# A graph layer's edge sums: 32-column strips placed by one matmul, and eight dense blocks instead of five

## The reference

```
x: (6250, 256); src, dst: 200000 edges, dst sorted; edge_weight
dst = int(6250 * u**2), u uniform; src uniform
xn = layernorm(x)
gnn:  xn @ W_self + segment_sum((xn @ W_neighbor)[src] * edge_weight, dst) + bias
mix:  linear attention: q, k, v = xn @ w_qkv (8 heads of 64), k and v normalised per head,
      out = q @ (k.T @ v) / N @ w_out + b_out
x = x + gnn + mix
x = x + ffn(layernorm(x))        # 8 experts, top 2, hidden 1024
```

## Time and profile before

| | |
|---|---|
| median of 3 runs | 2875.6 us (2859.43 to 2879.97) |
| span of the profiled execution | 2417.9 us |
| PE, PEld busy | 2142.0 us (89%), 1814.8 us (75%) |
| DVE, ACT, POOL busy | 1326.0 us (55%), 788.0 us (33%), 1489.1 us (62%) |
| DMA | 273.02 MB, mean 113 GB/s |

### The profile page before, as it was taken

One profiled execution on the slowest core, in us unless ns is written; L12 is line 12 of the kernel. 1 busy time (PEld: TensorE's weight loads), 2 busy tenths in 40 slices (PEclk: granted clock), 3 DMA queues, 4 the chain that ended last, 5 costly groups with the idle time before them and its releaser, 6 DMA issues. The chain is left out here.

```text
span 2417.9 us, 50110 instructions
## 1 busy us (share of the span) xinstructions
PE 2142.0 (89%) x11532; PEld 1814.8 (75%) x11533; DVE 1326.0 (55%) x3807; ACT 788.0 (33%) x2485; POOL 1489.1 (62%) x1637
## 2 busy tenths in 40 slices
PE   6699977887789989988988896958999999999998
PEld 5477766666677666766766685947999999999998
DVE  7788867465584776676577454683222222222222
ACT  4355524122341432332243000333333333333332
POOL 2377777777777777777777775013545545545544
PEclk9799999999999999999999998579999999999999
DMA  8533334643346335534634664761222222222222
GB/s 284 166 105 106 107 108 120 180 126 105 108 125 198 110 110 173 149 110 133 189 109 125 191 206 121 250 243 25 37 37 35 37 37 35 37 37 35 37 37 33
DMA packets 160182, 273.02 MB, mean 113 GB/s; under 512 B 29900, under 2 KB 115660, under 8 KB 159788
## 3 DMA queue, kind: packets, MB, share of 16 engines
q0 software_dynamic: 78480, 195.05, 30.8%
q1 hardware_dynamic: 81632, 77.16, 9.9%
HBM read 232.65 MB, written 39.45 MB: 113 GB/s over the span
## 5 line engine op out<-in xcount | busy, mean ns | idle before, releaser
L847 POOL DMA_INDIRECT big<-support_d,big x1088 | 1060.7, 975 | 323.7 <-issue 292.8
L1244 PE MATMUL psBB<-big 128*128 128x256 f32 x2176 | 556.8, 413 | 140.0 <-DMA big<-support_d,big 111.7
L1244 PEld LDWEIGHTS psBB<-big 128*128 128x128 f32 x2176 | 444.1, 207 | 251.5 <-issue 181.5
L1747 POOL DMA_INDIRECT out<-accs,sidx x104 | 233.8, 2248 | 294.1 <-DVE accs L1821 246.3
L1077 DVE TENSOR_SCALAR R_<-big 128x196 f32<-128x196 f32 x761 | 271.9, 393 | 107.1 <-PE psD L1275 84.5
L1046 DVE TENSOR_SCALAR big<-big 128x128 f32<-128x128 f32 x1088 | 296.0, 365 | 0.0
L1853 PE MATMUL psBB<-accs 128*128 128x128 f32 x1664 | 195.4, 276 | 0.0
L1853 PE MATMUL psC<-accs 128*128 128x128 f32 x1664 | 194.3, 275 | 0.0
L1853 PEld LDWEIGHTS psBB<-accs 128*128 128x128 f32 x1664 | 191.1, 193 | 0.0
L1853 PEld LDWEIGHTS psC<-accs 128*128 128x128 f32 x1664 | 190.0, 192 | 0.1
L1863 PE MATMUL psD<-big,accs 128*128 x832 | 188.2, 379 | 0.0
(11 more groups left out here) (324 smaller groups left out, 2861.6 us busy)
## 6 DMA issues: line engine op xcount, KB each, us to landing
big<-support_d SPq DMA_DIRECT2D x140, 128.0 KB
big<-support_d,big POOLq DMA_INDIRECT x1088
big<-w POOLq DMA_DIRECT2D x16, 1024.0 KB, 11.7
sup_s_<-support_d SPq DMA_DIRECT2D x105, 128.0 KB
big<-xnT_d SPq DMA_DIRECT2D x98, 128.0 KB
out<-accs SPq DMA_DIRECT2D x7, 896.0 KB, 4.2
xnT_d<-R_ SPq DMA_DIRECT2D x36, 128.0 KB, 1.9
accs<-x POOLq DMA_DIRECT2D x5, 896.0 KB, 10.6
```

What stands on the lines that cost most here:

```text
L847: nc.gpsimd.indirect_dma_start(out=G[:, s, t, :], out_offset=None, in_=support_d, in_offset=bass.IndirectOffsetOnAxis(ap=idxs[:, s * GT + ...
L1244: last = nc.tensor.matmul(psBB[:, bank, 0:D], S[:, s % SETS * GT + t, :], G[:, s, t, :], start=(t == 0), stop=(t == GT - 1))
L1747: nc.gpsimd.indirect_dma_start(out=out, out_offset=bass.IndirectOffsetOnAxis(ap=sidx[:, b.s:b.s + 1], axis=0), in_=y[:, b.s, :], in_offset ...
```

## The change

**Strips.** A group's eight columns of edges are four strips of two. Each strip spans fewer than 32 nodes, so its one-hot is 128x32 against the strip's own base node, and its product goes to 32 of the 128 output lanes. ScalarE copies the 128 x 256 result to SBUF (`take_group`), and one product with a 0/1 matrix (`spread`) puts the lanes in their places (`finish`), into the other bank. VectorE makes all eight one-hots in one comparison and one multiplication of 128x256. GpSimd now waits for `strips_done`, and the zero matmuls go. A group with a strip of 32 nodes or more, or 128 and more in all, is left out (its bases are moved by `ASIDE`) and summed column by column in a loop at the end, which runs once on padding if there is none.

**Tables.** The first stage finds lowest and highest node per strip and not per group (16 transposes instead of 4, 22 small products instead of 5, about 25 more operations on at most 98 x 8 elements); four passes over all 1568 columns that put the lanes apart go. The tables of windows have 256 entries instead of 160.

**Order.** 8 dense blocks instead of 5, with 6 rounds in block 0 and 3 in each other (one group in each turn, four at the end), 6 key/value tiles in each block and 7 in the last; then 1 round beside the mixing and the rest alone. ScalarE copies the group of a turn before it goes on with the columns of that turn's later windows.

```diff
-HEAVY = 5
+HEAVY = 8
-HALVES = ((0, 8, (2, 2)),)
-STAGES = ((0, 1, ((0, 8, (4,)),), 2, 6), (1, 2, ((0, 4, (4,)), (4, 8, (2, 2))), 2, 4), (2, HEAVY - 1, HALVES, 2, 3),
-          (HEAVY - 1, HEAVY, HALVES, 1, 3))
-ROUNDS_MIX = 2
+NARROW = 32
+STRIPS = P // NARROW
+SPLIT = GT // STRIPS
+KV_BLOCK = 6
+QUARTERS = ((0, 4, (1, 1, 1, 1), (1, 0, 1, 1)), (4, 8, (1, 1, 1, 1), (0, 1, 0, 1)))
+STAGES = ((0, 1, ((0, 6, (2, 2), (0, 1)), (6, 8, (4,), (1,))), 1, 6), (1, 2, QUARTERS, 1, 4), (2, HEAVY - 1, QUARTERS, 1, 3), (HEAVY - 1, HEAVY, QUARTERS, 2, 3))
+ROUNDS_MIX = 1
...
                         wait_apart(pool,
                                    (idx_ready, i * 2 + s // 2 + 1),
-                                   (group_used, i * RING + s + 1))
+                                   (strips_done, i * RING + s + 1))
...
+                def take_group(s, n):
+                    wait_apart(act,
+                               (strips_done, n + RING),
+                               (node_done, n))
+                    nc.scalar.activation(strips[:, s % SETS, :], strip_sums, ACT.Copy).then_inc(strips_taken, 1)
...
+                    if kt is not None:
+                        square(kt)
+                    for q in range(PER_TURN):
+                        if brings(sums, q):
+                            take_group(*groups.pop(0))
+                        if q == 1 and kt is not None:
+                            root(kt)
+                        while ahead <= min(q + 2, len(quads)) and (ahead - 1 <= q or not brings(sums, ahead - 1)):
+                            select_source(ahead % PER_TURN, u, *quads[ahead - 1])
+                            ahead += 1
+                        if q % 2:
+                            evict(b, q // 2, b * TURNS + j, j)
...
-                        for t in range(GT):
-                            c = s * GT + t
-                            nc.vector.tensor_scalar(S[:, s % SETS * GT + t, :], index[:, 0:P],
-                                                    cols[:, 0, c:c + 1], cols[:, 1, c:c + 1],
-                                                    ALU.is_equal, ALU.mult).then_inc(s_ready[t], 1)
+                def select_node(s, g, n, block, lane):
...
+                    dve.wait_ge(strips_done, n + RING - SETS)
+                    nc.vector.tensor_tensor(mine, iota[:, 0:NARROW].unsqueeze(1).to_broadcast(shape),
+                                            dst_wts[:, 0, bass.ds(c, GT)].unsqueeze(2).to_broadcast(shape),
+                                            ALU.is_equal).then_inc(found, 1)
+                    dve.wait_ge(node_done, n)
+                    nc.vector.tensor_scalar(spread[:, x, :], turning[:, bass.ds(within(dve.snap(turned), 1, P), P)], place[:, bass.ds(g + s, 1)], None,
+                                            ALU.is_equal).then_inc(spread_ready, 1)
+                    dve.wait_ge(found, n)
+                    nc.vector.tensor_tensor(mine, mine, dst_wts[:, 1, bass.ds(c, GT)].unsqueeze(2).to_broadcast(shape),
+                                            ALU.mult).then_inc(s_ready, 1)
...
+                def sum_group(s, full, n):
+                    pe.wait_ge(gathered[s], full)
+                    pe.wait_ge(strips_taken, pe.snap(n + SETS - 1))
+                    pe.wait_ge(s_ready, pe.snap(n))
+                    for i in range(SPLIT):
+                        for q in range(STRIPS):
+                            t = q * SPLIT + i
+                            last = nc.tensor.matmul(strip_sums[q * NARROW:(q + 1) * NARROW, :], S[:, s % SETS * GT + t, :],
+                                                    G[:, s, t, :], start=(i == 0), stop=(i == SPLIT - 1))
+                    last.then_inc(strips_done, 1)
+
+                def finish(s, full, n):
+                    pe.wait_ge(strips_taken, pe.snap(n + SETS))
+                    pe.wait_ge(spread_ready, pe.snap(n))
+                    pe.wait_ge(ps_free, pe.snap(n + 1))
+                    nc.tensor.matmul(node_sums, spread[:, s % SETS, :], strips[:, s % SETS, :],
+                                     start=True, stop=True).then_inc(node_done, 1)
```

More of the change, by code:

```diff
@@ L639, in _ @@
+                step(nc.vector.tensor_reduce(rall[:, 1:2], wide, AX.X, ALU.add))
+                step(nc.vector.tensor_scalar(mtab[0:1, GROUPS + 1:], rall[:, 1:2], 1.0, None, ALU.max))
                 norms(25, 28)
@@ L929, in _ @@
+                rounds = within(act.snap(act.snap(ROUNDS - r0) & MASK), LIGHT_LEAST, ROUNDS)
+                with act.Fori(ROUNDS_HEAVY, rounds) as r:
+                    for group in groups_from(r):
+                        take_group(*group)
             @block.vector
@@ L1236, in sum_group @@
-                def sum_group(s, full, first, end):
-                    with pe.Fori(first, end) as n:
-                        own = pe.snap(n + 1)
-                        pe.wait_ge(ps_free, own)
-                        bank = within(odd(n), 0, 1)
-                        pe.wait_ge(gathered[s], full)
-                        for t in range(GT):
-                            pe.wait_ge(s_ready[t], own)
-                            last = nc.tensor.matmul(psBB[:, bank, 0:D], S[:, s % SETS * GT + t, :],
-                                                    G[:, s, t, :], start=(t == 0), stop=(t == GT - 1))
-                        last.then_inc(pair_used, 1)
@@ L1248, in free_group @@
[L1248 to L1254 removed]
+                    return [(s, full, r * RING + s + 1) for s in range(RING)]
```

563 lines of the change are left out of this document (352 added, 211 removed).

## The result

The changed kernel is slower: 3016.9 us (median of 4 runs, 3016.4 to 3024.0) beside 2872.9 us for the kernel before, ratio 1.0525, interval 1.0487 to 1.0563. The forecast was 2800 us.

The account below looks back on a forecast made before the run. GpSimd's indirect gathers (1.286 us each) were taken to bound the graph stage. Graph stage -84 us, tail +6 and first stage +2 gave -76, so 2875.6 us became about 2800, range 2715 to 2900.

Parts of the forecast that it names:

- 457.7 more: Whole run: median 2875.6 us less profiled span 2417.9 us, taken to lie around the span and stay unchanged.
- -76 us: Whole kernel: graph stage -84 us, behind the last gather +6, first stage +2; span from 2417.9 to 2342 us.
- Gathers removed: Graph stage on GpSimd: 960 gathers instead of 1088 at 1.286 us, -164.6 us if GpSimd kept its pace.
- Strips: TensorE, per group of 1024 edges: eight strip products partly overlapping in 1.95 us, 2.7 us with waits, copy and placement.
- The turn: Later dense blocks: 12.9 us with a key/value tile, 8.05 without, 11.1 on average, 11.3 taken; a block 133 us.
- Who sets the pace: Later dense blocks: turns of 11.3 us where gathers want 10.3; GpSimd waits for strip products some 10 us a block.
- gathers keep their pace: Rival, graph stage: the forecast's chains are too long and GpSimd stays the bound, 2725 us; chance 0.13.
- The other stretches: Graph stage: block 0 268 us, block 1 150, six blocks 798, light groups 99; 1315 us against 1399.2.
- Before and behind: First stage +2 us, bounds -5 and +8; behind the last gather +6 us for copy, placement and the wide-group loop.
- Serial strips: Rival, TensorE: each strip product uses the array alone, 3.46 us a group, 156 us in all, 2956 us; chance 0.2.
- All four at once: Rival, TensorE: strip sums take the 0.87 us bound, a block 129 to 130 us, 2765 us; chance 0.12.
- Lock-step over ScalarE: Rival: TensorE waits 1 to 1.5 us more per turn for columns behind ScalarE's copy, 2865 to 2895 us; chance 0.1.

Follow-up runs that it names:

- even series: Kernels run after each other on one chip, where the unedited kernel before takes 2417 to 2424 us; the profile behind the prediction is like one.
- held: Kind of series in which the unedited kernel before takes 2810 to 2880 us and register and branch instructions of several engines are slow.
- half gathers: Kernel before with every other gather left out from the second round on: 2243.0 us beside 2421.7, and 2288.4 us beside 2822.5 in the slower kind of series.

## Why the prediction was wrong, point by point

**The step that failed** is the last of the sum: "457.7 more, which lies around the span and isn't changed". One profiled execution stood 16% under the median of the runs, and its stage of gathers was taken for that of the runs. The section on the time and profile before says the same of the runs' times, and both are wrong: in every run since, a span is its run's time less 1 to 3 us. The gap of a sixth was itself the hint that the profile was of another kind of execution. The rest of the sum, -76 us, was right in its sign where it can be tested: in an even series the change gave -45.4 us (2373.8 - 2419.2). The forecast was therefore of another execution than the one measured, and none of the rivals had in it that all engines could be held up. A block then costs what it costs with its streams held: 59 to 79 us on top in a later block of the changed kernel, 50 to 61 in one of before.

Why before loses less per block can be read off the half gathers: its other engines need 175 us for a block and its gathers 203 to 205, so up to 30 us of delay are hidden in every block; in the changed kernel they need 124 and the gathers 3 x 32 x 1.286 = 123.5, and nothing is. 55 + 30 = 85 against 77: the delay itself is about the same per block. This is argued from these lengths, not tested by itself.

**Gathers removed: right.** 960 of them, 1.286 us each as before. Even, the stage from first to last gather went from 1398.2 to 1339.2, -59.0 where -84 was forecast.

TensorE's waits for their data went from 111.7 to 65.1 us, none of it in blocks 1 to 7.

**Strips: wrong in size, on the good side.** 1.95 us was assumed. TensorE of the changed kernel, even, a turn with a key/value tile in order of time:

```profile
842.76 1.07 PE L1431 MATMUL psBB<-big 128*32 128x256 f32 x16
843.96 0.17 PE L1444 MATMUL psD<-zeros 128*128 128x1 bf16 x1
844.31 1.26 PE L1461 MATMUL psD<-R_,big 128*128 128x196 f32 x6 [0.18 <-issue]
845.40 0.60 PE L1439 MATMUL psBB<-big 128*128 128x256 f32 x2
...
847.61 1.26 PE L1461 MATMUL psE<-R_,big 128*128 128x196 f32 x6 [0.40 <-ACT big L1005]
849.18 1.26 PE L1461 MATMUL psE<-R_,big 128*128 128x196 f32 x6 [0.32 <-ACT big L1005]
...
854.81 1.07 PE L1431 MATMUL psBB<-big 128*32 128x256 f32 x16
```

Sixteen records in 1.07 us where the earlier trace rows has 3.63: all four strips run at once, the bound of 0.87 and a little. The Trainium skill (TensorEngine Tiling (Array Packing), Tiling Modes) has this, and the trace agrees; of the drain at each change of mode that the page also names, the trace shows at most the 0.13 us between the strips' end and the next product.

**The turn: 12.0 us with a tile (842.76 to 854.81) where 12.9 was forecast.** The waits for ScalarE's columns are there (0.40 and 0.32) and small. ScalarE's copy was right (0.38), VectorE's broadcasts too (0.42 and 0.43 against 0.44). A later block came to 124.2 instead of 133.

**Who sets the pace.** The forecast had GpSimd wait some 10 us a block for strip products. In the last five blocks it waits 3.0, 2.3, 0.3, 1.2 and 2.0 us, and four of them are as long as their gathers (123.5 us): there the rival "gathers keep their pace" was right. With half of the gathers such a block takes the same 124 us, so the other engines' chain happens to be equally long, and the forecast's 133 us for it was too long. GpSimd's waits for the strips, 111.3 us in the whole stage, lie elsewhere: 26.8 in block 0, 5.1 in block 1, 32.3 in block 2 (which has 39 turns of three columns and took 152.9 us) and 38.2 behind the last block.

**The other stretches, even.** Block 0 took 290.0 us, 22 more than forecast; its window tables were priced right (two operations of 4.4 us). Block 1 147.5 (150), the six others 781.5 (798), the rest 121.1 (99): there GpSimd is not "at pace" but waits for TensorE, which sums a group only between two lots of 25 mixing tiles:

```profile
ACT big L989 <- PE psBB L1431: 118.9, 11, 28.1
DVE accs L1166 <- PE psBB L1439: 45.6, 9, 9.4
POOL big L938 <- PE psBB L1431: 38.2, 4, 18.6
```

That is the table of waits from 1322 to 1443 us; one wait of GpSimd is 18.6 us long. Blocks 0 and the rest give back +44, the six blocks and block 1 take 19.

**Before and behind.** The first stage was put at +2 us with a bound of +8: the first gather starts at 102.9 instead of 94.5, +8.4. Behind the last gather, from its start to the last add, 9.8 us instead of 13.0; from there to the first expert output 168.6 instead of 161.7, the +6 forecast for the loop over wide groups. Sum: -59.0 + 8.4 - 3.2 + 6.9 = -46.9 us, against -76.

**Rivals.** Serial strips: no. All four at once: yes as a mechanism; it was to give 2765. Gathers keep their pace: in the later blocks, not over the stage. Lock-step over ScalarE: about 10 us a block, held, and only at a block's end; its reading of the earlier trace rows has a slip, since the fifth block's clock of 0.94 stood beside TensorE busy for 88% of the time and not 85%. A reader of the result alone might take it for one of the two that forecast 2865 or more (serial strips, lock-step); it was neither.

**What stays open.** What in a gather holds up the other engines' register instructions, and why only in some series. It shows only where gathers and dense blocks run together: at the end of the stage gathers go out beside the mixing with next to no slow instruction, and the experts' stage has as many instructions, 36 GB/s of transfers and none at all. Many transfers by themselves aren't enough: right behind the last gather, held, 197 GB/s are moved without a slow instruction. Whether the gather's instruction or its rows matter wasn't seen, since the run that would have told came even. Nor is it known whether these instructions run slowly or arrive late; the two runs on the length of loop bodies test only that length. A page of the Trainium skill (NOTIFIC — the notification-queue block, Overflow: three behaviours, one of which stalls the engine) says that the block which writes an engine's notification records can hold the engine up when its own pipeline backs up; that would fit a cause common to several engines, but GpSimd, whose records go there too, has next to no slow instruction, and no run here tests it.

No version beats both kernels in both kinds of series: six and eight blocks are 2% ahead of before even, and in a held series the strips with five blocks are the best that was measured (0.7%). Six blocks weren't seen held.

## What to carry to other kernels

Before anything is priced from a profile, its span has to match the runs that will be the measure; where it is a sixth shorter, find the missing time first. A plan that trades a slower-looking engine's work for more instructions on all the others is only worth its price where those instructions cost what the profile says, and slack behind the bound is worth something when they don't. And when an engine's pace seems to set a block, take half of its work away once: it shows how far behind the next bound is (30 us in before, none in the changed kernel).

## What the runs showed of the hardware

- Register and branch instructions of ScalarE, VectorE and SyncE can take 0.70 us instead of 0.03 to 0.24, singly or in a row of up to 17.7 us, in step across the engines (350 of 394 pairs of starts a multiple of 0.70 us apart), while compute instructions keep their durations (ScalarE's one-hot columns 0.40 us, a gather 953 ns); 368 to 544 us of a graph stage with all gathers and loads lay in such stretches. GpSimd had none to 5 of them.
- With half of the indirect gathers (one run) they went from 675 (ScalarE, VectorE, SyncE and TensorE) to 152, and the kernel from 2822 to 2288 us, where the same edit is worth 179 us in an even series.
- Four 32-column strips of fp32 products side by side: 16 records in 1.07 us, against 3.63 for 16 on all columns.
- An indirect gather of 64 rows of 1 KB costs GpSimd 1.246 us, one of 128 rows 1.286.
- A loop body of four times the length (the pairs of turns of a block written out) cost 0.4%.
